# Sorted experts with their stores behind two row loads, a third row buffer, and a norm moved to ScalarE in a two-layer decoder kernel

## The reference, cut to what matters

```
x = x + attention with a relative bias, 16 heads         (layer 0)
x = x + cross attention to 64 context rows in 4 windows, 8 heads
x = x + mixture of 8 experts, best 2 per row
x = x + attention in groups of 32, FFN, regrouped, attention, FFN   (layer 1)
x = x + cross attention with rotary positions, norm, FFN
x = x + mixture of low-rank experts, best 2 per row
```

```
rms = mean(xf * xf);  normed = bf16(xf * rsqrt(rms + eps) * norm_weight)
logits = bf16(normed @ gate.T + bias);  scores, idx = top_k(logits, 2);  w = softmax(scores)
p1 = normed @ mlp1[e] + b1[e];  g = min(p1[0::2], 7);  lin = clip(p1[1::2], -7, 7)
act = g * sigmoid(1.702 g) * (lin + 1);  p2 = act @ mlp2[e] + b2[e]
out = xc + bf16(sum over the two experts of w * p2)
```

## Time and profile before

| what | value |
|---|---|
| time, median of 3 runs | 2193.9 us (2191.62 to 2198.99) |
| the profiled execution, its own time | 2199.73 us |
| its span, first to last instruction | 2197.9 us |
| PE busy | 1906.6 us (87%) |
| DVE, ACT, POOL busy | 1303.5, 971.4, 966.4 us |
| mean granted PE clock | 0.930 |
| HBM read and written | 77.14 and 39.85 MB |

### The profile page before, as it was taken

One profiled execution on the slowest core, in us unless ns is written; L12 is line 12 of the kernel. 1 busy time (PEld: TensorE's weight loads), 2 busy tenths in 40 slices (PEclk: granted clock), 3 DMA queues, 4 the chain that ended last, 5 costly groups with the idle time before them and its releaser, 6 DMA issues.

```text
span 2197.9 us, 52542 instructions
## 1 busy us (share of the span) xinstructions
PE 1906.6 (87%) x21476; PEld 1579.2 (72%) x21476; DVE 1303.5 (59%) x2964; ACT 971.4 (44%) x1952; POOL 966.4 (44%) x783
## 2 busy tenths in 40 slices
PE   7999999999999999666355528999999999998994
PEld 5677777777777777455244427999989999987883
DVE  6767676667677666267522336555556545555883
ACT  3666666666666665311222203424334423424551
POOL 2555555555555555245311162334334334344441
PEclk9999999999999999898566658999999999999996
DMA  7001020102311001342211142000022010031000
GB/s 261 16 18 56 11 80 11 56 28 112 119 38 49 11 11 39 123 144 73 74 46 44 55 144 84 12 21 13 12 85 73 17 31 17 17 119 28 11 16 15
DMA packets 75149, 120.37 MB, mean 55 GB/s; under 512 B 8424, under 2 KB 65008, under 8 KB 71536
## 3 DMA queue, kind: packets, MB, share of 16 engines
q1 hardware_dynamic: 69504, 102.68, 14.0%
q0 software_dynamic: 2560, 6.30, 1.0%
q10 hardware_dynamic: 2848, 8.04, 1.0%
HBM read 77.14 MB, written 39.85 MB: 53 GB/s over the span
## 4 chain that ended last, share of the span: by engine, by line
PE 40%; DMA 5%; DVE 5%; issue 4%; POOL 2%; SPq 2%; ACT 2%; POOLq 0%; DVEq 0%; ACTq 0%
PE psum L265 12%; PE psum L276 8%; PE psum L1999 4%; PE psum L1987 2%; DMA b_xs<-xs 2%; PE psum L2491 2%; PE psum L225 2%; PE psum L1333 2%; PE psum L1973 2%; PE psum L2525 1%; PE psum L1350 1%; PE psum L1243 1%; DMA b_x_in<-in_x 1%; PE psum L246 1%; ACT e_pr L2630 1%
## 5 line engine op out<-in xcount | busy, mean ns | idle before, releaser
L770 POOL TENSOR_TENSOR a_sm<-a_sm,a_rsum 128x1024 f32<-128x1024 f32 x256 | 479.9, 1894 | 356.7 <-DVE a_rsum L804 354.3
L792 DVE CUSTOM_DVE_ANT_0 a_sm<-psum,a_strip 128x1024 f32<-128x1024 f32 x256 | 312.0, 1219 | 146.6 <-PE psum L624 146.6
L705 ACT ACTIVATE a_sm<-a_sm,a_mn 128x1024 f32<-128x1024 f32 x256 | 293.9, 1148 | 28.2 <-DVE a_mn L792 26.9
L637 PE MATMUL psum<-ident,a_sm 128*128 128x128 f32 x2048 | 275.2, 277 | 5.2 <-POOL a_sm L770 4.2
L710 ACT ACTIVATE a_pT<-psum 128x512 f32<-128x512 f32 x256 | 151.6, 592 | 273.0 <-PE psum L637 273.0
L637 PEld LDWEIGHTS psum<-ident,a_sm 128*128 128x128 f32 x2048 | 223.8, 140 | 62.7 <-issue 46.0
L652 PE MATMUL psum<-a_pT,a_V 128*64 128x256 f32 x2048 | 249.0, 385 | 0.6 <-ACT a_o L716 0.6
L652 PEld LDWEIGHTS psum<-a_pT,a_V 128*64 128x64 f32 x2048 | 136.1, 136 | 77.3 <-issue 22.1
L799 DVE COPY a_pT<-psum 128x512 f32<-128x512 f32 x256 | 174.9, 683 | 12.2 <-PE psum L637 4.9
L2083 ACT ACTIVATE g_val<-psum 128x512 f32<-128x512 f32 x64 | 38.1, 597 | 217.7 <-PE psum L1999 217.7
L624 PE MATMUL psum<-a_KH,a_QH 64*128 64x512 f32 x512 | 114.7, 445 | 2.5 <-DVE a_mn L792 2.5
(11 more groups left out here) (393 smaller groups left out, 3946.5 us busy)
## 6 DMA issues: line engine op xcount, KB each, us to landing
a_strip<-table SPq DMA_DIRECT2D x16, 960.0 KB, 6.8
oT<-a_o SPq DMA_DIRECT2D x64, 128.0 KB, 1.9
xs<-b_zeros SPq DMA_DIRECT2D x8, 1024.0 KB, 4.1
b_oT_in<-oT SPq DMA_DIRECT2D x8, 1024.0 KB, 6.4
y<-b_yb SPq DMA_DIRECT2D x23, 256.0 KB, 2.1
b_xs<-xs SPq DMA_DIRECT2D x23, 128.0 KB, 2.2
a_raw<-in_a_wqkv SPq DMA_DIRECT2D x7, 384.0 KB, 3.3
s_x<-in_x_rev SPq DMA_DIRECT2D x4, 512.0 KB, 7.4
```

The lines of the kernel that those rows point to most:

```text
L637: last = pe.transpose(psum[:, 4 + j, k * P:(k + 1) * P], sm[:, st % RING, kt * P:(kt + 1) * P], ident[:, :])
L705: a.activation(sm[:, st % RING, :], sm[:, st % RING, :], ACT.Exp, scale=-1.0, bias=mn[:, at:at + 1], accum_out=rsum[:, at:at + 1]).then_in ...
L770: g.tensor_tensor(sm[:, st % RING, :], sm[:, st % RING, :], rsum[:, at:at + 1].broadcast_to([P, T]), ALU.mult).then_inc(sig("scaled"), 1)
L792: v.tensor_tensor_reduce(out=sm[:, st % RING, :], in0=scores_banks(hl).rearrange("p c n -> p (c n)"), in1=strip[:, pair % 2, hl, qt * P:qt ...
```

## The change

Six things are changed, in the two functions.

1. SP loads tile j + 3, then stores the result of unit j - 2 (before: of unit j); the loop runs two iterations more.
2. The rows of the cross attention get a third slot, which lies over the tiles of the sorted experts; `fetch(s)` waits for the joining of chunk s - 3. Its semaphores are those of the sorted tiles, which count on from 4. The context loads stand one chunk later.
3. The expert weights are issued by SP, behind the rows of chunk 1 (b1) and of chunk 2 (w2, w1). ACT widens w2 in round 4 and fills `pick` in round 5; the loads of the next step's queries stand behind all row loads.
4. The norm of chunks 1 to 7 ahead of the cross attention is two ACT passes, scale times x plus an offset per row; POOL works the offset out (minus the mean, times the root; two operations on 128x2).
5. The squares of each chunk are two ACT passes with an accumulator.
6. The first two chunks' x3 is written into the rows of the next step, and is not loaded back. `first_stats`, `first_norm` and `low_columns` stand behind the first, second and third combination, `first_root` behind the second gather.

```diff
@@ cross_and_mixture @@
+    third_at = nc.sbuf_base - 2 * UR * PT * D * 2
     yb = sb("yb", [P, UR, PT, D])
+    slots.append([nc.alloc_sbuf_tensor_at("b_oT_in2", [P, HP, CP], F32, offset=third_at),
+                  nc.alloc_sbuf_tensor_at("b_x_in2", [P, PT, D], F32, offset=third_at + HP * CP * 4)])
...
-    weights = [("w2b", w2b[:, :, :, :], A["m_w2"]), ("w2b", b1b[:, :, :, :], A["m_b1"]),
+    weights = [("b1", b1b[:, :, :, :], A["m_b1"]), ("w2b", w2b[:, :, :, :], A["m_w2"]),
                ("w1", w1[:, :, :, :].rearrange("p k e n -> p k (e n)"), A["m_w1"])]
...
-            sp.wait_ge(sig("ay_out"), s - 1)
-            oT, x, _, _ = slots[s % 2]
+            if s > 2:
+                sp.wait_ge(sig("ay_out"), s - 2)
+            oT, x = slots[s % 3][:2]
...
         def store(s):
             r = s % 2
+            rows = then["rows"][:, s, :, :] if s < 2 else x3[:, r, :, :]
...
         load_rows(sp, have, 1, mixture_rows(A, S, slots, 1))
+        load_weights(sp, have, weights[:1])
+        fetch(2)
         fetch_context(2)
-        for s in range(2, NP):
+        load_weights(sp, have, weights[1:])
+        for s in range(3, NP):
             fetch(s)
-            if s + 1 < NP:
-                fetch_context(s + 1)
-            if s == 4:
-                sp.wait_ge(sig("wide"), 2)
-                then["load_queries"](sp)
+            if s > 3:
+                fetch_context(s - 1)
+        fetch_context(NP - 1)
+        sp.wait_ge(sig("wide"), 2)
+        then["load_queries"](sp)
         sp.wait_ge(sig("tables"), 1)
         sp.wait_ge(routed("sc"), 16 * 2 * PT * NP)
         for j in range(UR):
             fetch_sorted(j)
         then["load_projections"](sp)
-        for j in range(NU):
+        for j in range(NU + 2):
             if j + UR < NU:
                 fetch_sorted(j + UR)
-            store_sorted(j)
+            if j >= 2:
+                store_sorted(j - 2)
         for s in range(NP):
             store(s)
-            if s == 1:
-                for r in range(2):
-                    sp.wait_ge(sig(f"st{r}"), 16 * (1 + P // SEG))
-                then["load_first"](sp)
...
@@ scalar @@
-        load_weights(a, have, weights)
...
-            if r == 0:
+            if r == 4:
+                a.wait_ge(have("w2b"), 16)
                 a.activation(w2[:, :, :, :], w2b[:, :, :, :], ACT.Copy).then_inc(sig("wide"), 1)
-            if r == 1:
+            if r == 5:
                 a.wait_ge(sig("made"), 8)
...
             if 0 < s < NP:
+                a.wait_ge(sig("bn_off"), 2 * s)
+                a.wait_ge(sig("bT_ps"), s)
+                for t in range(PT):
+                    a.activation(h[:, t, :], x1[s % 2][:, t, :], ACT.Identity, scale=bn[2][:, t:t + 1],
+                                 bias=offset[:, t:t + 1]).then_inc(sig("bn_h"), 1)
                 a.wait_ge(sig("bT_ps"), s + 1)
...
+            if 0 <= b < NP:
+                for t in range(PT):
+                    a.wait_ge(sig("mn_h"), PT * b + t + 1)
+                    if b:
+                        a.wait_ge(sig("m_normed"), PT * b)
+                    a.activation(junk[:, t, :], xc[:, b, t, :], ACT.Square, accum_out=ss[:, t:t + 1]).then_inc(sig("m_ss"), 1)
@@ gpsimd @@
-        first_sum(1)
...
+        first_sum(1)
...
             if s < NP:
+                g.wait_ge(sig("bn_var"), PT * (s + 1))
+                g.wait_ge(sig("bn_h"), PT * s)
+                g.tensor_scalar(offset[:, :], bn[1][:, :, 0], -1.0, None, ALU.mult).then_inc(sig("bn_off"), 1)
                 norm_rstd(g, sig, "bn", s, bn, mhalf)
+                g.wait_ge(sig("bn_off"), 2 * s - 1)
+                g.wait_ge(sig("bn_rstd"), s + 1)
+                g.tensor_tensor(offset[:, :], offset[:, :], bn[2][:, :], ALU.mult).then_inc(sig("bn_off"), 1)
...
             gather(s)
-            if s == 3:
+            if s == 1:
                 then["first_root"](g)
@@ vector @@
             norm_apply(v, sig, "mn", s, x2[:, s, :, :], xc[:, s, :, :], mn)
-            for t in range(PT):
-                v.wait_ge(sig("mn_h"), PT * s + t + 1)
-                if s:
-                    v.wait_ge(sig("m_normed"), PT * s)
-                v.scalar_tensor_tensor(junk[:, t, :], xc[:, s, t, :], 1.0, xc[:, s, t, :], ALU.mult, ALU.mult,
-                                       accum_out=ss[:, t:t + 1]).then_inc(sig("m_ss"), 1)
...
-            v.tensor_tensor(x3[:, r, :, :], x2[:, s, :, :], mo[:, :, :], ALU.add).then_inc(sig("x3"), 1)
-
-        v.wait_ge(have("w2b"), 16 * 2)
+            rows = then["rows"][:, s, :, :] if s < 2 else x3[:, r, :, :]
+            v.tensor_tensor(rows, x2[:, s, :, :], mo[:, :, :], ALU.add).then_inc(sig("x3"), 1)
+
+        v.wait_ge(have("b1"), 16)
...
-            if s < NP:
-                v.wait_ge(sig("bT_ps"), s)
-                norm_apply(v, sig, "bn", s, x1[s % 2], h, bn)
...
-        for s in range(3):
-            combined(s)
+        combined(0)
         then["first_stats"](v)
+        combined(1)
+        then["first_norm"](v)
+        combined(2)
+        then["low_columns"](v)
         combined(3)
-        then["first_norm"](v)
         combined(4)
-        then["low_columns"](v)
         combined(5)
```

More of the change, by code:

```diff
@@ L1163, in loaded @@
         else:
[L1164 removed]
+            eng.wait_ge(sig(f"lx{s % 3}"), 16 * 2 * ((s - 2) // 3 + 1))
     def loaded_context(eng, s):
@@ L1242, in attended @@
             for k in range(HP):
-                last = pe.matmul(bank[:, t * D:(t + 1) * D], slots[s % 2][0][:, k, t * P:(t + 1) * P], wo[:, k, :],
+                last = pe.matmul(bank[:, t * D:(t + 1) * D], slots[s % 3][0][:, k, t * P:(t + 1) * P], wo[:, k, :],
                                  start=k == 0, stop=k == HP - 1)
@@ L1859, in loaded @@
         if s < 2:
-            eng.wait_ge(have(f"rows{s}"), 16)
+            eng.wait_ge(before["signals"][0]("x3"), s + 1)
         elif local(s):
```

37 lines of the change are left out of this document (16 added, 21 removed).

## The result

The changed kernel takes 2054.8 us (median of four runs, 2052.1 to 2065.7) against 2196.4 beside it: ratio 0.937, 95% interval 0.933 to 0.940, 142 us less. Run once more against nine runs of the kernel before it gave 2053.6 us and 0.936 (0.934 to 0.938). The forecast was 2058, with a range of 2040 to 2100.

The account below looks back on a forecast made before the run. PE waits in three stretches (cross attention, sorted experts, combination); the later stage is bound by matmuls. Experts 103, cross attention with its start 18.6 and combination 14.5 make 136 us, from 2193.9 to 2058; range 2040 to 2100.

Parts of the forecast that it names:

- Experts: Sorted experts: stores behind two loads hide each tile's load; 20 units go from 8.47 to 3.3 us, gain 103 us.
- turning a tile adds at most 0.61: Experts' unit on PE: 2.72 us for up and down plus at most 0.61 for the turn, 3.3 us.
- The rival of a slow PE: Experts' stage: PE stays at clock 0.67, a unit costs 4.56 us, gain 78, total 2083 us; chance 0.12.
- that of a late load: Experts' stage: the load stays one unit behind, about half the wait remains, total 2101 us; chance 0.05.
- The start: Cross attention's start: with weights behind the rows, rows arrive at 911.5 and not 917.85, 6.3 us gained.
- Heavy rounds: Cross attention, four rounds with a next chunk: 19.4 us each fall to 16.7, gain 10.8 us.
- The norm on ACT: Cross attention's rounds: moving the norm's two passes from DVE to ACT adds 0.9 us a round.
- The squares: Cross attention's rounds: moving two passes of squares off DVE's path saves 0.76 us per chunk.
- The third buffer: Cross attention's rows: saves only what a row load is late beyond the chunk sum DVE must take out of the bank.
- Tables in each round: Rival, cross attention: ACT switches tables between exponential and square, 20.5 us in eight rounds, total 2079; chance 0.10.
- The combination: Combination of the experts' rows: PE starts the next stage at about 1286.5 and not 1301.30, 14.5 us gained.
- The later stages: Matmul stage from 1345 us: untouched; rival with a lower clock, at 0.80 170 us more, 2228; chance of slower 0.02.

Follow-up runs that it names:

- norm_dve: The changed kernel with the cross attention's norm back on VectorE and GpSimd's two offset operations gone: 2062.1 us, ratio 0.939; eight chunk sums 98.5 us.
- rows_late: The changed kernel with a chunk's row loads issued only when the chunk two before is joined, as with two buffers: eight chunk sums 103.3 us.
- one_behind: The kernel before with only the store of unit j-1 put behind the load of unit j+3: 2098.1 us against 2194.8, ratio 0.956.
- stores_only: The kernel before with only the store of unit j-2 put behind the load of unit j+3: 2087.5 us against 2194.8, ratio 0.950.
- squares_dve: The changed kernel with the squares back on VectorE: eight chunk sums 107.3 us.
- both_dve: The changed kernel with both norm and squares back on VectorE: eight chunk sums 106.3 us.

## Why the prediction was right, and where its steps were off

- **Experts, 103 us predicted: right, a little small.** From the turn of tile 3 to the up of unit 22 it is 59.8 us for 169.3, 109.5 less. The step that was off is "turning a tile adds at most 0.61": that was a turn's whole duration, in a stage at 0.67 (0.38 to 0.40 in the changed kernel). A unit with its turn takes 2.99 us, against the 2.72 without, so the turn adds 0.27. The condition that PE binds held, and the load is on PE with room to spare. The rival of a slow PE is refuted by the clock of 0.97 to 0.99, that of a late load by three waits.
- **The start, 6.3: right in its cause, a little small.** From the issue of the rows to PE's first product 6.95 us (906.99 to 913.94) for 14.4, so 7.5, just over the bound of 7.3. The self-attention ahead of it ended 3.5 us later in this profile than in that of before.
- **Heavy rounds, 16.7 us each: right in the sum, not in its make-up.** They take 16.95 and 16.3 in the two profiles. The prediction let them go from 18 (with the still-stand) to 15.9 (without) and took the middle; measured are 17.3 to 18.2 with and 14.7 to 15.1 without. So the 16.7 is an average over how many rounds have one, two or three of four, and that it was met is in part luck. What the prediction missed is what goes with it: the "5.34 us product" was taken as a fixed duration, with 15.3 us "if PE's clock is up" as an aside (15.9 less the whole 1.6 us between 5.34 and 3.7 is 14.3). In all 15 cases the slow product stands ahead of the still-stand.
- **The norm on ACT, +0.9 a round:** in rounds without a still-stand 14.7 to 15.1 with it and 13.5 in two of norm_dve's without, so 1.2 to 1.6 (its third such round took 14.6; in it DVE lost 1.2 us on one instruction beside POOL's second sum). Each pass took 590 ns, the pair 1.08 us: the Trainium skill's figure for it (ScalarE: Activation LUTs, What ACT_TABLE_LOAD costs) fits, and the 0.94 from the gate's row was too low. The trace shows it:

```profile
L1423 ACT ACTIVATE b_h<-b_x1b,b_offset,b_bn_rs 128x256 f32<-128x256 f32 x8 | 4.3, 590 | 22.8 <-POOL b_offset L1506 22.8
...
L1440 ACT ACTIVATION_READ_ACCUMULATOR b_junk<-b_xc 128x1 f32 x16 | 3.0, 186 | 0.0
```

- **The squares, -0.76:** 0.6 a round between profiles with two still-stands each; the sign is right, the size a little large.
- **The third buffer:** taken as what "a row load is late beyond this sum". rows_late puts it at 0.2 us. "Late beyond this sum" was true of four products of the kernel before (17.0 us of waits), but the cause was not the number of buffers: the context loads, and once the query loads, stood in front of the rows in SP's list. The prediction named neither as a gain; its 12.3 us for the rounds, got mostly from the average of two lengths, came out near the measured 11.7 to 14.9 for the whole stretch by luck as much as by reasoning. The weights' new place gave the start alone, as it said.
- **Tables in each round:** refuted. The whole trace has five table loads, none among the rounds.
- **The combination, 14.5: the step failed though its number was met.** The first product came 14.2 us sooner, but "these move up as much", said of the last combinations and the key products, does not hold: they are paced by the gathers, and the products that start sooner wait for DVE's key copies. By itself the seam is worth 5.8 us (1 to 10). In the changed kernel the second chunk's turn comes 7.4 to 7.9 us sooner than in one_behind and stores_only, and 13.8 sooner than in the profile of before, with its further stops.
- **The later stages:** as predicted, no slower for the clock (0.96 to 0.97).

The total came out within 4 us because the experts' term was 6 us short and the seam's, by itself, some 8 us long. That the two errors nearly cancel is luck.

## What to carry to other kernels

In a queue that works in order, count the distance of a load from the wait ahead of it in microseconds of its consumer's pace, and look at single units: here a distance that was too short by one unit made every second unit wait, not each. Read the rest of such a queue's list in the same way: a load whose own buffer is free still waits behind a load whose buffer is not. When the start of a stage is moved up, look for what paces its middle before its gain is booked. And where an engine's record shows a tiny operation at microseconds, look at what the other engine on the same port does, and at what made it arrive just then.

## What the runs showed of the hardware that I had not expected

- PE's granted clock fell for single products: the same 16 matmuls take 3.70 us behind others and 5.1 to 5.4 us behind 1.9 to 3.6 us of idling, yet 3.69 us behind 1.9 to 2.7 us of it in five cases (norm_dve at 977.67 and 992.31, squares_dve at 965.01 and 998.95, both_dve at 998.30). What decides between the two these runs don't show.
- Two POOL sums back to back (1.28 and 1.27 us) keep DVE out for both: 2.8 to 3.2 us in the changed kernel and its variants for an operation of 0.17 to 0.19.
- PE products coming one by one, with 7.4 to 13.2 us of stops in seven of the fourteen profiles, with nothing to wait for in the trace; absent in both profiles of the changed kernel, and present in kernels that differ from it elsewhere and ran on other chips. It is as large as what most of the edits here were meant to gain.
